# Graph attention stage: scores kept in PSUM with a relu on ScalarE and a subtraction on GpSimd, and weighted sums laid out row by row

## The reference

```python
def gat_layer(x, adj, W, a_self, a_neigh, b):     # x [N,F], adj [N,N], W [H,F,32]
    feat = jnp.einsum('nf,hfo->hno', x, W)
    attn_self = jnp.einsum('hno,ho->hn', feat, a_self)
    attn_neigh = jnp.einsum('hno,ho->hn', feat, a_neigh)
    e = attn_self[:, :, None] + attn_neigh[:, None, :]
    e = jax.nn.leaky_relu(e, 0.2)
    e = e + MASK_VAL * (1.0 - adj)[None, :, :]    # MASK_VAL = -1e10
    alpha = jax.nn.softmax(e, axis=-1)
    out = jnp.einsum('hnm,hmo->hno', alpha, feat) + b[:, None, :]
    out = jnp.transpose(out, (1, 0, 2)).reshape(out.shape[1], -1)
    return jax.nn.elu(out)
# h = gat_layer(ctx_512, layernorm(x), W0, ...);  x = x + gat_layer(h, layernorm(x), W1, ...)
```

## Time and profile before

| What | Value |
|---|---|
| Three timed runs, us | 1275.07, 1279.4, 1282.12 (median 1279.4) |
| The profiled execution's own time | 1281.72 us |
| Its span in the profile | 1279.9 us |
| Busy over the span | PE 86%, DVE 70%, ACT 46%, POOL 29% |
| First `edges` matmul of the stage | 25.26 us |
| End of the last addition to x (L1345) | 235.76 us |

### The profile page before, as it was taken

How to read it: one execution, slowest core, us unless ns; L and a number is a source line. 1 busy time by engine, 2 the same in 40 slices (tenths; PEclk the granted TensorE clock), 3 DMA queues, 4 the chain that set the end, 5 groups by cost and what they waited for, 6 DMA issues and landing times.

```text
span 1279.9 us, 20454 instructions
## 1 busy us (share of the span) xinstructions
PE 1103.1 (86%) x6058; PEld 871.2 (68%) x6058; DVE 892.0 (70%) x2599; ACT 588.6 (46%) x1525; POOL 367.8 (29%) x291
## 2 busy tenths in 40 slices
PE   7988898419999317898989898998998999999998
PEld 3645555415666206787878787787888888888887
DVE  4688777615776186886488558846872878878877
ACT  5556546103333104895389357935873322222221
POOL 1656545040000332322132223313210233323331
PEclk9978776658999756999999999999998999999999
DMA  8900000111111210101010101010000111111111
GB/s 254 318 1 2 1 1 1 61 66 37 47 46 47 65 50 0 43 1 34 1 41 1 33 1 41 0 33 1 2 25 14 38 43 43 49 49 49 49 41 41
DMA packets 55555, 53.36 MB, mean 42 GB/s; under 512 B 5520, under 2 KB 48976, under 8 KB 55488
## 3 DMA queue, kind: packets, MB, share of 16 engines
q1 hardware_dynamic: 53952, 48.38, 12.2%
q0 software_dynamic: 1536, 4.20, 1.0%
HBM read 43.38 MB, written 9.18 MB: 41 GB/s over the span
## 4 chain that ended last, share of the span: by engine, by line
PE 68%; DVE 11%; issue 10%; ACT 8%; POOL 1%; DMA 1%; SPq 1%; DVEq 0%; ACTq 0%; POOLq 0%
PE bank L54 12%; PE bank L55 11%; PE bank L56 11%; PE bank L565 4%; PE bank L812 4%; PE bank L792 3%; PE bank L696 3%; PE bank L704 3%; PE bank L721 3%; ACT prob L1049 2%; PE bank L548 2%; DVE g_scale L1323 2%; PE bank L804 2%; PE bank L814 2%; PE bank L534 2%
## 5 line engine op out<-in xcount | busy, mean ns | idle before, releaser
L1222 POOL TENSOR_TENSOR rot_s<-swap,rq 128x512 f32<-128x512 f32 x64 | 82.7, 1291 | 273.7 <-ACT swap L1037 272.6
L1049 ACT ACTIVATE prob<-prob,pmin 128x128 f32<-128x128 f32 (+1 forms) x256 | 114.2, 448 | 74.4 <-DVE pmin L1620 72.9
L792 PE MATMUL bank<-kv,norm 128*128 128x128 f32 (+1 forms) x512 | 112.2, 345 | 13.8 <-DVE norm L1605 10.7
L957 ACT ACTIVATE silu<-bank 128x512 f32<-128x512 f32 x66 | 39.5, 599 | 178.0 <-PE bank L56 178.0
L1518 DVE SCALAR_TENSOR_TENSOR xs<-bank,wt,xs 128x256 f32<-128x256 f32 x264 | 109.0, 475 | 0.0
L1172 POOL TENSOR_TENSOR gate_r<-gate_w,gate_r 128x256 fp32r<-128x256 f32 x33 | 38.8, 1177 | 232.3 <-ACT gate_r L943 232.3
L1632 DVE TENSOR_SCALAR prob<-prob,pinv 128x128 f32<-128x128 f32 (+1 forms) x256 | 99.2, 430 | 4.6
L1154 POOL TENSOR_SCALAR rest<-alpha 128x512 f32<-128x512 f32 x32 | 69.8, 2182 | 80.0 <-ACT alpha L889 78.7
L812 PE MATMUL bank<-probT,kv 128*128 128x256 f32 x256 | 83.5, 409 | 9.3 <-ACT probT L1059 8.4
L792 PEld LDWEIGHTS bank<-kv,norm 128*128 128x128 f32 x512 | 71.1, 199 | 21.1 <-issue 13.7
L1620 DVE CUSTOM_DVE_ANT_0 prob<-bank,causal 128x128 f32<-128x128 f32 (+1 forms) x256 | 80.0, 350 | 7.3 <-issue 5.1
(11 more groups left out here) (237 smaller groups left out, 3074.8 us busy)
## 6 DMA issues: line engine op xcount, KB each, us to landing
gate_w<-in_Wg SPq DMA_DIRECT2D x33, 128.0 KB, 2.2
up_w<-in_Wu SPq DMA_DIRECT2D x33, 128.0 KB, 2.3
down_w<-in_Wd SPq DMA_DIRECT2D x33, 128.0 KB, 2.3
w_all<-in_w_gate SPq DMA_DIRECT2D x8, 512.0 KB, 9.3
w_all<-in_w_up SPq DMA_DIRECT2D x8, 512.0 KB, 9.2
w_all<-in_w_down SPq DMA_DIRECT2D x8, 512.0 KB, 9.3
wq_g<-in_Wq SPq DMA_DIRECT2D x4, 1024.0 KB, 5.4
wq_g<-in_Wo SPq DMA_DIRECT2D x4, 1024.0 KB, 5.6
```

Source lines behind the costliest of these rows:

```text
L792: mm = pe.matmul(S_BANK[k % 2][:, nt * P:nt * P + (nt + 1) * P], qT[:, h % 2, b * N + nt * P:b * N + nt * P + P], kT[:, b * N:b * N + (nt ...
L1049: ins = act.activation(prob[:, k % 4, nt * P:nt * P + (nt + 1) * P], prob[:, k % 4, nt * P:nt * P + (nt + 1) * P], ACT.Exp, bias=pmin[:, k ...
L1222: signal(pool.tensor_tensor(rot_s[:, half].rearrange("p (b n) -> p b n", b=2), swap[:, half].rearrange("p (b n) -> p b n", b=2), bcast(tab ...
```

## The change

- **Scores.** `edges` on PE now goes round three banks. ACT no longer copies z; it writes `excess = relu(-4 z)` to SBUF for every unit, the terms having been multiplied by 0.2 beforehand (two small DVE instructions in `prepare_vectors`). GpSimd makes `bias - excess` for every unit, with one instruction. DVE's instruction with the minimum now reads z from PSUM and that sum from SBUF. `leak` and the two GpSimd instructions of the odd units are gone. A bank of z is free when DVE's instruction is done (`edge_done`), no longer when ACT has copied it.
- **Weighted sums.** In `weigh` `alphaT` is now the stationary operand (128 columns), and the features of one head with a column of ones behind them (33 columns) move. For a quad there are again 16 matmuls, and all write one bank. The result stands with nodes on partitions. The reciprocal is of 128x8 sums.
- **Bias.** The layer's bias is added to the features, by one more matmul in every `features` call: one row of ones against the bias row.
- **Turning.** Layer 1's result is now transposed (`turn_h1`, two transposes for a quad, and a copy `copy_h1` on ACT), and layer 2's is not; DVE adds it to x straight away, in two instructions for a quad. `turn_x1` and `add_x1` are gone.

```diff
@@ PE
-                    if k >= 2:
-                        pe.wait_ge(S["z_copied"], k - 1)
-                    pe.matmul(ZB[k % 2]...
+                    if k >= 3:
+                        pe.wait_ge(S["edge_done"], k - 2)
+                    pe.matmul(ZB[k % 3]...
@@ features, after the matmuls over c
+                    mm = pe.matmul(FEAT[:, nt * D:nt * D + D], one_row[:], bias_row[:, r // B, :], start=False, stop=True)
@@ weigh
-                    for cols, w in ((slice(0, N), lambda mc, h: feat[r % 2][:, mc, h * GO:(h + 1) * GO]),
-                                    (slice(N, 2 * N), lambda mc, h: one_w[:])):
-                        for mc in range(NT):
-                            for h4 in range(QUAD):
-                                mm = pe.matmul(OB[j % 2][h4 * GO:(h4 + 1) * GO, cols], w(mc, QUAD * c + h4),
-                                               alphaT[:, j % 2, h4, mc, :], start=mc == 0, stop=mc == NT - 1)
+                    for nt in range(NT):
+                        for h4 in range(QUAD):
+                            at = (nt * QUAD + h4) * (GO + 1)
+                            for mc in range(NT):
+                                mm = pe.matmul(OB[:, at:at + GO + 1], alphaT[:, j % 2, h4, mc, nt * P:nt * P + P],
+                                               feat[:, r % 2, mc, QUAD * c + h4, :], start=mc == 0, stop=mc == NT - 1)
+                def turn_h1(j):
+                    pe.wait_ge(S["g_elu"], j + 1)
...
+                    for nt in range(NT):
+                        mm = pe.transpose(MISC[:, N + nt * P:N + nt * P + P], hid1[:, j % 2, nt * P:nt * P + P], ident[:])
@@ ACT
-                    act.activation(alpha[:, k % RING, :], ZB[k % 2][:], ACT.Copy, scale=NEG if k % 2 else 1.0)
+                    act.activation(excess[:, k % 2, :], ZB[k % 3][:], ACT.Relu, scale=1.0 - 1.0 / NEG)
+                def copy_h1(j):
+                    act.activation(h1T[:, r, c, :], MISC[:, N:2 * N], ACT.Copy)
@@ GpSimd, each k
-                if k % 2:
-                    pool.tensor_scalar(rest[:], alpha[:, k % RING, :], 1.0 / NEG - 1.0, 0.0, ALU.mult, ALU.min)
-                    pool.tensor_tensor(alpha[:, k % RING, :], alpha[:, k % RING, :], rest[:], ALU.add)
+                pool.tensor_tensor(alpha[:, k % RING, :], adj[:, k // UNITS % B]..., excess[:, k % 2, :], ALU.subtract)
@@ DVE
-                    dve.scalar_tensor_tensor(alpha[:, k % RING, :], alpha[:, k % RING, :], NEG, alpha[:, k % RING, :],
-                                             ALU.mult, ALU.min)
-                            in0=alpha[:, k % RING, nt * N:nt * N + N], in1=adj[:, r % B, nt, :], ...
+                            in0=ZB[k % 3][:, nt * N:nt * N + N], in1=alpha[:, k % RING, nt * N:nt * N + N], ...
-                    chain.link(dve.reciprocal(g_scale[:], OB[j % 2][:, N:2 * N]))
+                    chain.link(dve.reciprocal(rsum[:], sums[:, :, :, GO]))
-                    dve.tensor_tensor(rows, FEAT[:], rows, ALU.add)
+                    dve.tensor_tensor(rows, g_pos[:, j % 2, :]..., rows, ALU.add)
```

More of the change, by code:

```diff
@@ L317, in build @@
         ALLQ = ROUNDS * QUADS
-        LAST = ALL + 11
+        LAST = ALL + 9
         def starts_in(k, lead):
@@ L338, in alphaT_copied, with prepared_before, turned_before @@
             return S["alphaT_dve" if copied_by_dve(k) else "alphaT_act"], len(mine)
+        def prepared_before(k):
+            return sum(r == 0 or UNITS * r - 4 <= k for r in range(ROUNDS))
+        def turned_before(k):
+            return sum(4 * j + 13 < k for j in range(B * QUADS))
         def copied_by_dve(k):
@@ L518, in features @@
                         pe.wait_ge(S["feat_copied"], r)
-                    if nt == 0 and r >= B + 3:
-                        pe.wait_ge(S["x1_added"], r - B - 2)
                     ks, src = sources(r)
                     for c in range(ks):
-                        mm = pe.matmul(FEAT[:, nt * D:nt * D + D], src(c)[:, nt * P:nt * P + P],
-                                       w0[:] if r < B else w1[:, c, :], start=c == 0, stop=c == ks - 1)
+                        pe.matmul(FEAT[:, nt * D:nt * D + D], src(c)[:, nt * P:nt * P + P],
+                                  w0[:] if r < B else w1[:, c, :], start=c == 0, stop=False)
+                    mm = pe.matmul(FEAT[:, nt * D:nt * D + D], one_row[:], bias_row[:, r // B, :], start=False, stop=True)
                     mm.then_inc(S["feat_ready"], 1)
@@ L595, in graph_attention @@
                         weigh(j)
-                    if (r := round_at(k, 17)) is not None:
-                        turn_x1(r)
+                    if (j := quad_at(k, 4)) is not None and j < B * QUADS:
+                        turn_h1(j)
             def turn_norm(which, w=None):
@@ L915, in exp_out @@
                         act.wait_ge(S["g_elu"], j)
-                    act.activation(g_exp[:], g_out[:, j % 2, :], ACT.Exp, bias=bT[:, layer, c:c + 1]
-                                   ).then_inc(S["g_exps"], 1)
+                    act.activation(g_exp[:], g_out[:, j % 2, :], ACT.Exp).then_inc(S["g_exps"], 1)
+                def copy_h1(j):
+                    r, c = divmod(j, QUADS)
+                    act.wait_ge(S["h1_ready"], j + 1)
+                    act.activation(h1T[:, r, c, :], MISC[:, N:2 * N], ACT.Copy).then_inc(S["h1T_copied"], 1)
                 copy_features(0)
@@ L928, in graph_attention @@
                         exp_out(j)
+                    if (j := quad_at(k, 5)) is not None and j < B * QUADS:
+                        copy_h1(j)
                     if (r := starts_in(k, 1)) is not None:
@@ L1149, in _ @@
             for k in range(ALL):
-                if k % 2:
[L1151 to L1158, removed]
+                pool.wait_ge(S["z_relu"], k + 1)
+                if k % UNITS == 0 and k < B * UNITS:
+                    pool.wait_ge(S["adj_bias"], k // UNITS + 1)
+                if k >= RING:
+                    pool.wait_ge(S["alphaT_ready"], k - RING + 1)
+                pool.tensor_tensor(alpha[:, k % RING, :], adj[:, k // UNITS % B].rearrange("p u n -> p (u n)"),
+                                   excess[:, k % 2, :], ALU.subtract).then_inc(S["z_less"], 1)
                 if (r := starts_in(k, 4)) is not None and r < B:
@@ L1260, in prepare_vectors @@
                 chain.link(dve.memset(wst1[:], 0.0))
-                dve.memset(one_w[:], 1.0)
+                dve.memset(one_row[:], 1.0)
+                dve.memset(feat[:, :, :, :, GO:], 1.0)
                 heads = lambda ap: ap.rearrange("p (h o) -> p h o", h=GH)
@@ L1268, in prepare_vectors @@
                         chain.link(dve.tensor_reduce(wst1[:, c, at:at + GH], heads(wa_tmp[:, 2 + 2 * c + j, :]), X, ALU.add))
+                chain.link(dve.tensor_scalar(wst0[:, 0:2 * GH], wst0[:, 0:2 * GH], NEG, None, ALU.mult))
+                chain.link(dve.tensor_scalar(wst1[:, :, 0:2 * GH], wst1[:, :, 0:2 * GH], NEG, None, ALU.mult))
                 chain.link(dve.tensor_copy(wst0[:, ROW:], wst0[:, 0:2 * GH]))
                 chain.link(dve.tensor_copy(wst1[:, :, ROW:], wst1[:, :, 0:2 * GH]))
-                dve.tensor_scalar(bT1[:], bT[:], -1.0, None, ALU.add)
                 dve.tensor_copy(ind[:], ind_f[:]).then_inc(S["wa_done"], 1)
@@ L1292, in prep @@
                                       ALU.subtract).then_inc(S["st_copied"], 1)
-                def leak(k):
-                    dve.wait_ge(S["z_copied"], k + 1)
-                    dve.scalar_tensor_tensor(alpha[:, k % RING, :], alpha[:, k % RING, :], NEG, alpha[:, k % RING, :],
-                                             ALU.mult, ALU.min).then_inc(S["z_dve"], 1)
                 def edges(k):
                     r, h = divmod(k, UNITS)
-                    dve.wait_ge(S["z_pool" if k % 2 else "z_dve"], k // 2 + 1)
-                    if h == 0 and r < B:
-                        dve.wait_ge(S["adj_bias"], r + 1)
+                    dve.wait_ge(S["z_less"], k + 1)
                     for nt in range(NT):
                         ins = dve.tensor_tensor_reduce(
-                            out=alpha[:, k % RING, nt * N:nt * N + N], in0=alpha[:, k % RING, nt * N:nt * N + N],
-                            in1=adj[:, r % B, nt, :], scale=1.0, scalar=3.0e38, op0=ALU.add, op1=ALU.min,
+                            out=alpha[:, k % RING, nt * N:nt * N + N], in0=ZB[k % 3][:, nt * N:nt * N + N],
+                            in1=alpha[:, k % RING, nt * N:nt * N + N], scale=1.0, scalar=3.0e38, op0=ALU.add, op1=ALU.min,
                             accum_out=edge_min[:, k % RING, nt:nt + 1])
@@ L1351, in graph_attention @@
                         edges(k - 2)
-                    if 0 <= k - 1 < ALL and (k - 1) % 2 == 0:
-                        leak(k - 1)
                     if 0 <= k - 5 < ALL and copied_by_dve(k - 5):
@@ L1363, in graph_attention @@
                         elu(j)
-                    if (r := round_at(k, 18)) is not None:
```

(5 more changed lines are left out.)

99 lines of the change are left out of this document (47 added, 52 removed).

## The result

| | Kernel before | Changed kernel |
|---|---|---|
| Median time, us | 1277.76 (4 runs, 1275.07 to 1282.12) | 1366.53 (4 runs, 1355.73 to 1374.55) |
| Profiled execution, us (span) | 1281.72 (1279.9) | 1368.6 (1366.8) |
| End of the last addition to x, us | 235.76 | 327.29 |

The ratio is 1.0686, with a 95% interval of 1.0603 to 1.0768: slower by 6.9%. The stage ends 91.5 us later; all that follows it takes 4.6 us less (1366.8 - 327.3 = 1039.5 against 1279.9 - 235.8 = 1044.1), though the change leaves that code alone. Most of this goes with the scores path: in the traces of all twelve kernels of this document, what follows the stage takes 1043.1 to 1044.1 us in the three with the old scores path (before, `sums_only`, `wide_dve_bias_old_scores`) and 1038.5 to 1040.5 in the nine with the new one. Why, no run shows.

A forecast was written before the change was run, and what follows sets the result against it. PE at 1.2 GHz was taken to bound the attention stage: 302 us of work plus 1.7 fill, 2.0 end and 0.4 start, 306 against 210.5, +96; less 10 for spells, +86, so 1366 us. The 8-in-10 range was 1302 to 1384.

The forecast's parts named there:

- Which stage and what bounds it: Graph attention alone, 210.5 us of the span; at 1.2 GHz PE never waits and is the chain's only member.
- The weighing, +3.2 us a quad: A quad's 16 matmuls at 1.2 GHz: 32 loads at 0.213 us, 6.8 us against 3.6, +52 us for 16.
- The bias matmul, 0.85 us: One more 256-column matmul in each of 16 features calls, priced as a layer 1 features call: +13.6 us.
- `turn_h1`, 0.52 us a quad: Two transposes for each of 8 quads, half of 1.05 us: +4.2 us, offset by `turn_x1` going, -4.2.
- Nothing on the other engines is late: DVE, ACT and GpSimd chains stay hidden behind PE at 1.2 GHz; at 2.4 GHz 0.3 to 1 us stall a quad.
- my signs of being wrong: New weighing's records 0.12 us apart or less, grant at 1.00 through weighings, or PE waiting for `edge_done`.
- The filling of the pipeline, the start and the end: Added to PE's work in the stage: fill about 1.7 us, end 2.0, small instructions and a memset before it 0.4.
- The 302 us of PE's work: PE's work in the stage after the change, all at 1.2 GHz, against 237 us before.
- The clock: The old weighings that preceded each rise go, so nearly all the stage runs at 1.2 GHz; chance 0.65.
- the two spells allowed: Layer 2's features call and bias together may bring the clock up; two spells of 7 us, -10 us.
- The swings of before: Rival: the stage's clock swings as before, 0.57 of the work at 2.4 GHz; +27 us, 1307 us, chance 0.15.
- 2.4 GHz for an engine without gaps: Rival: gapless PE gets 2.4 GHz all through the stage; -22 us, 1258 us, chance 0.10, 0.07 with a gain.

The follow-up runs named there:

- `sums_only`: The changed kernel with the old scores lines put back, its three banks for z kept: 1365.86 us, ratio 1.0633.
- `wide_dve_bias_old_scores`: `wide_whole` with the bias added by DVE as it copies the features out of PSUM, and the old scores path put back: 1270.49 us, ratio 0.9943.
- `no_bias_matmul`: The changed kernel without the bias matmul in the features calls, so the result lacks the bias: 1350.44 us, ratio 1.0568.
- `wide_whole`: The changed kernel with 132 moving columns in each weighing matmul instead of 33, every head's result kept: 1285.3 us, ratio 1.0066.
- `dense_filler`: The changed kernel with four more f32 matmuls of 248 moving columns, results unread, before each weighing: 1385.23 us, ratio 1.0852.

## Why the prediction was right

- *Which stage and what bounds it.* Held. PE is alone in the chain, and taking 18.4 us from it took 16 from the time.
- *The weighing, +3.2 us a quad, from narrow matmuls of another stage.* Held: 6.97 us measured against 6.8, in 16 weighings 2.7 us more. At 2.4 GHz it was priced at 4.0 by the ratio of a step, and is 3.90.
- *The bias matmul, 0.85 us.* Too low: 1.15 us, so 18.4 and not 13.6. I had priced it as 256 moving columns alone. In the timeline its first load starts only as the features matmul before it ends, at 107.05, where the load of a features call (105.79) starts well within the matmul before it:

```profile
106.98 0.49 PEld L527 LDWEIGHTS bank<-bias_row,one_row 1*128 1x128 f32 x2 [0.65 <-issue]
```

A load takes about 0.28 us there, which is the 0.30 us that was missing; why this load is not done ahead, no run shows. The layer 1 features call that I took for it keeps its 0.85 us.
- *`turn_h1`, 0.52 us a quad.* It costs 0.48, and the transposes behind it 0.85 where they are 1.04 otherwise, so 0.3: 2 us less over 8 quads.
- *Nothing on the other engines is late.* Held at 1.2 GHz once the pipeline is full: PE's waits for `edge_done`, one of my signs of being wrong, are 2.5 us, and both lie in the filling.
- *The filling of the pipeline, the start and the end.* Too low. The first edges come at 26.59 us instead of 25.26, 1.3 us later and not 0.4 (two bias matmuls of 1.15 us stand ahead of them), and the first transposes after the fill at 35.4 us instead of 32.1. In the stage PE stands idle for 300.7 - 294.3 = 6.4 us, where the sum had 1.7 + 2.0; 1.9 us of it lie before the last two weighings' transposes and loads, where it had nothing.
- *A term counted wrongly.* The 302 us of PE's work hold the first round's prep, features and bias matmuls, 1.0 + 1.7 + 1.7 = 4.4 us in the prediction's prices, and these run before the first edges, so before the stage as it was measured. This made the forecast too high.
- *The clock.* Held, and it is what decides: the forecast's 1.2 GHz for nearly all of the stage. Of the two spells allowed one came, of 7.6 us, in layer 2 as named, but not from what was named: it began behind a prep, before the features call and the bias, and in `no_bias_matmul` such spells came without any bias matmul. By the chain's own prices its work would have cost 13.4 us at 1.2 GHz, so it gave back 5.8, not 10.
- *The number is partly luck.* The measured time is higher than the terms say by 2.7 (weighings), 4.2 (the 14 bias matmuls in the stage), 4.2 (spells), 2.7 (idle time) and 0.9 us (start), and lower by 1.8 (turning), 4.4 (the first round) and some 3 us of small things, such as transposes of 0.91 us behind the weighings of layer 2. So the stage ends 91.5 us later where 86 were forecast, and the 4.6 us of the later stages, which no term had, bring 1366.5 next to 1366.
- *The swings of before* (1307 us) did not come: no weighing of 33 columns was followed by a rise of its own. With 99 or 132 columns they came, at 1287 and 1285 us; that rival's price was 20 us too high. It had PE busy for 231 us with 5 to 8 us of stalls and ends; in `wide_whole` PE is busy for 201 us and idle for 17, so more of the work went at 2.4 GHz and PE waited more.
- *2.4 GHz for an engine without gaps* (1258 us) did not come, as 27 to 60 us of the kernel before had said. PE is busy 12.00 of 12 us in window after window at 2.19 us a step. The Trainium skill ("TensorE: Matmul & The Clock Gate", section "Why this matters for your kernels") asks only that TensorE be kept busy without gaps; here that did not do, and the measurement decides.

Of the stage's 91.5 us, then, PE's added work at 1.2 GHz is 16 x (6.97 - 3.6) + 18.4 - 2 = 70 us. The clock, an estimate, adds 47: before, it saved PE 53 us (the 237 of the prediction less the first round's 2.7, against 181 measured), after only 6. Against these stand the waits that are gone: PE was idle for 210.5 - 181.2 = 29.3 us and is for 6.4, so 23. That is 94 us for a measured 91.5.

## What to carry to other kernels

Price a reshaped matmul by its loads at both clocks, from rows of like shape anywhere in the trace, and then ask what it was doing for the clock: whether the stretches that came before each rise are still there. Where the load sets the spacing, moving more columns than are needed cost next to nothing (7.02 us for 66 columns against 6.97 for 33 at 1.2 GHz, 3.80 for 132 against 3.90 at 2.4 GHz), and it won 81 us back (1366.5 to 1285.3). Work saved on engines that wait for TensorE is turned into waiting.

## What the runs showed of the hardware that I had not expected

- The grant fell with PE busy all the time, right behind a stretch of 33-column matmuls (213 us of `dense_filler`, 229 us of the changed kernel). In the kernel before, the falls I had looked at came after an idle microsecond.
- Between 66 and 99 moving columns, with the same loads, the time falls by 61 us; from 99 to 132 by 2.
- Every rise seen in a 33-column kernel without filler, three in two traces, came right behind a prep of layer 2 and the transposes after it. Not every such prep was followed by one, and why some are is open.
- DVE's instruction with the minimum took 420 ns on average in the changed kernel, with z read from PSUM, against 519 before with both inputs in SBUF. Its median before is 420 ns too: the mean is raised by 24 of 128 that took over 450, up to 1521 ns, and each of these overlapped a GpSimd instruction. None of the 38 that ran with GpSimd idle was long, and 66 that overlapped were not either. The Trainium skill ("SBUF — State Buffer", section "Who interferes with whom") has a VectorE instruction with two SBUF inputs contend with GpSimd's reads; the traces agree. The saving of 13 us of DVE's time did nothing for the kernel's.
- Repeated runs of the changed kernel spread over 1.4% (1355.7 to 1374.6), those of the kernel before over 0.6% in the four runs beside them. One spell more or less is worth about 6 us. The trace of `sums_only` has none (1376.04 us) where that of the changed kernel has one (1368.6), which fits; that the spread comes from their number I have not shown.
